# Second cross-attention: smaller packs first, one combined normalisation, row tile 0 projected first, and each quad's queries made inside the loop

## The chip, the cores and the metric

One Trainium2 chip, and of it one core. The time is microseconds (us) of device time of one launch; a lower one is better. Five engines work from queues of their own, each in program order, and meet only at semaphores: PE (TensorE, matmuls), DVE (VectorE), ACT (ScalarE), POOL (GpSimd) and SP (SyncE, which here only issues DMAs and waits).

## What is computed

A perceiver block with x of shape (16, 64, 256) and a context of shape (16, 1601, 256). It has six stages in a row: a top-k cross-attention, a retention stage, a mixture-of-experts feed-forward, a **second cross-attention**, random features, and a tree-routed feed-forward. Only the second cross-attention is touched:

```python
def _L1_xattn_ref(q, k, v, norm_w, norm_b, norm1_w, norm1_b, Wq, bq, Wk, bk, Wv, bv, Wo, bo):
    B, L, D_MODEL, H = (4, 512, 256, 16)
    E = D_MODEL // H
    ...
    qn = layernorm(q, norm_w, norm_b)
    kn = layernorm(k, norm_w, norm_b)
    vn = layernorm(v, norm_w, norm_b)
    Q = (qn @ Wq + bq).reshape(b, l, H, E)
    K = (kn @ Wk + bk).reshape(b, s, H, E)
    V = (vn @ Wv + bv).reshape(b, s, H, E)
    scale = 1.0 / jnp.sqrt(jnp.asarray(E, Q.dtype))
    scores = jnp.einsum('blhe,bshe->bhls', Q, K)
    A = jax.nn.softmax(scale * scores, axis=-1)
    O = jnp.einsum('bhls,bshd->blhd', A, V)
    O = O + Q
    out = jnp.transpose(O, (0, 2, 1, 3)).reshape(b, l, H * E)
    return layernorm(out, norm1_w, norm1_b) @ Wo + bo + out
```

It is called with `_layernorm(x)` as q, so the queries pass two layer norms in a row, and with the context as both k and v.

## The kernel before

**Tiling.** The stage is the function `phase_heads_read`. x lies as 8 row tiles of 128 rows (NT = 8, D = 256, KD = 2 halves of D). There are B = 16 batches of L = 64 query rows each; a batch's context of S = 1601 rows is cut into four quarters (`SPANS`, 512, 384, 384 and 322 columns) and 13 chunks of up to 128 rows. The 16 heads go in two halves m = 0, 1 of 8 heads; one (batch, m) is a **quad**, n = 2b + m, 32 in all. In a quad four groups j of two heads each are worked on.

**What a quad needs.** A matmul of two fp32 factors is made exact enough from a high and a low part. `stage` holds keys as high and low; `load_stack` has SP copy them into `stack` by 12 DMAs, three for each j (high, low, high, 32 partitions each), and copy the queries (high, high, low) from the DRAM tensor `queries` into the tile `queries` by 3 DMAs. Both tiles have two slots, chosen by m. PE then runs 16 `find_top` matmuls (L1485; four spans for each j), DVE reduces each to a maximum (`take_top`, L1733), and the 4 x 128 maxima come back by `shift` (L1492) and `take_shift` (L1748) as four extra rows of the queries; the rows at partitions 96 to 99 of the stack are marks that select them. After that come 13 `score` chunks (L1503), `exp` on ACT (L1637) into `ring`, sums of the ring on POOL (L1389) and DVE (L1762), and `weigh` (L1519).

**Order of the loop.** It is written out by hand, in seven groups g of two chunks. While quad n is scored, PE finds the tops of quad n+1 (`TOP_AT`: in g = 2, 3, 4) and makes keys and values of the next batch (`fill`, L1462 and L1470, spread by `FILL_AT`). `find_top` v = 0 waits for all three queries DMAs; v = 0, 4, 8, 12 wait for the three stack DMAs of their j. SP runs `batch`: `load_stack(b, 1)` (which waits for all scores of the quad before, whose slot it is free to write one quad on), `load_rows(b + 2, 3)`, `load_stack(b + 1, 0)`, the row scales (`load_stds`) and three quarters of rows three batches ahead. SP is in order too: a wait holds back all DMAs behind it.

**Opening.** One DMA brings all parameters (`pd`, 2328 columns). DVE and ACT run the first norm (`d_ln0`), the weights of keys and values are scaled, centred and split, and the second norm (`d_ln1`) runs over the result of the first. PE then transposes all 8 tiles (L164), fills run, and after fill 1 all tiles are projected at once (L216). ACT and DVE build the masked, halved queries of all 16 batches in two pieces (`by_head(ownH)`, L1677, and `by_head(ownL)`, L1812); `ownH` sits in slot 1 of `stack`, `ownL` in `ring`. SP stores both (2 x 2 MB) to DRAM, waits for them, copies the marks and calls `load_stack(0, 0)`. Only then come the 16 first `find_top`s and the loop.

## Time and profile before

| | us |
|---|---|
| median of 3 runs | 1737.65 |
| their lowest and highest | 1735.89, 1746.78 |
| the profiled execution | 1746.88 |
| its span | 1745.0 |
| PE busy in the span | 1479.3 |
| DVE busy | 1032.5 |
| ACT busy | 644.8 |
| POOL busy | 611.9 |

The profile is of one execution, and its span begins with that execution's first work; a time such as 602.97 is us from there. The second cross-attention opens at 517.76 (first DMA), its first exponential starts at 602.97, and the last load of a quad is issued at 1391.13. TensorE's clock has two levels here, 1.2 and 2.4 GHz, shown as a share: 0.50 and 1.00. A row of a timeline gives start, duration, engine, line and operation, how many instructions are merged, and in brackets how long the engine was idle before and what ended that.

### The profile page before, as it was taken

To read this page: it belongs to the slowest core of one execution; us is meant where nothing else is said; L and a number is where in the kernel's file an instruction comes from. 1 tells how busy PE (TensorE), PEld (TensorE's weight loads), DVE (VectorE), ACT (ScalarE), POOL (GpSimd) and SP (SyncE) were. 2 spreads that over 40 slices of the span, in tenths; PEclk is the share of its full clock that TensorE was granted. 3 is DMA by queue.
4 is the path that set the end of the run, shared out by engine and by line. 5 is a ranking of instruction groups with operands and counts; after the bars stand their busy time and mean duration, and the time that the engine had idled before them with its cause. 6 is when DMAs were issued, how large, how long until landed. Compare 5 with 4: busy or idle time off the path is not lost. (4 is left out here: it accounts for less than half of the span.)

```text
span 1745.0 us, 29559 instructions
## 1 busy us (share of the span) xinstructions
PE 1479.3 (85%) x11422; PEld 1150.0 (66%) x11422; DVE 1032.5 (59%) x1937; ACT 644.8 (37%) x1210; POOL 611.9 (35%) x478
## 2 busy tenths in 40 slices
PE   7878767848945799999999999999999983669997
...
GB/s 358 175 260 274 235 1 91 191 1 1 193 40 101 249 140 159 123 148 180 157 143 162 138 143 157 162 132 167 108 151 123 78 47 63 61 109 1 1 0 24
DMA packets 100390, 220.09 MB, mean 126 GB/s; under 512 B 10065, under 2 KB 73889, under 8 KB 98721
## 3 DMA queue, kind: packets, MB, share of 16 engines
...
## 5 line engine op out<-in xcount | busy, mean ns | idle before, releaser
L1637 ACT ACTIVATE d_ring<-psum 128x512 f32<-128x512 f32 (+1 forms) x416 | 229.3, 595 | 301.9 <-PE psum L1503 229.1
L1389 POOL TENSOR_TENSOR d_ring<-d_ring 128x512 f32<-128x512 f32 x224 | 293.2, 1309 | 121.8 <-ACT d_ring L1637 105.5
L1733 DVE TENSOR_REDUCE d_top<-psum 128x1 f32<-128x400 f32 (+2 forms) x512 | 270.1, 569 | 101.4 <-PE psum L1485 96.7
L1503 PEld LDWEIGHTS psum<-d_queries,d_stack 100*128 100x128 f32 (+1 forms) x1664 | 212.0, 196 | 35.3 <-issue 34.5
L1503 PE MATMUL psum<-d_queries,d_stack 100*128 100x128 f32 (+1 forms) x1664 | 233.0, 284 | 1.0 <-DVE d_queries L1748 0.9
L1485 PE MATMUL psum<-d_stack,d_queries 96*128 96x400 f32 (+1 forms) x512 | 185.4, 419 | 40.9 <-DVE d_top L1733 31.9
L1356 POOL TENSOR_TENSOR d_rowsT<-d_raw,d_rowsT 128x1024 fp32r<-128x1024 f32 (+1 forms) x64 | 126.5, 1980 | 199.8 <-ACT d_rowsT L1608 199.8
L1470 PE MATMUL psum<-d_wv,d_rowsT 128*128 128x256 f32 (+1 forms) x1248 | 175.2, 292 | 7.3 <-DVE d_stage L1724 7.3
L1470 PEld LDWEIGHTS psum<-d_wv,d_rowsT 128*128 128x128 f32 (+1 forms) x1248 | 167.3, 194 | 7.9 <-DVE d_stage L1724 7.9
L1724 DVE SCALAR_TENSOR_TENSOR d_stage<-psum,d_bk,d_stage 128x384 fp32r<-128x384 f32 (+2 forms) x128 | 81.0, 633 | 143.0 <-ACT d_stage L1617 143.0
L1462 PE MATMUL psum<-d_rowsT,d_wk 128*128 128x384 f32 (+2 forms) x768 | 160.5, 359 | 3.0 <-POOL d_rowsT L1356 2.5
L1485 PEld LDWEIGHTS psum<-d_stack,d_queries 96*128 96x128 f32 x512 | 92.0, 200 | 92.7 <-DVE d_top L1733 75.7
L1519 PE MATMUL psum<-d_ring,d_val 128*32 128x128 f32 (+1 forms) x3328 | 151.2, 290 | 1.8 <-ACT d_ring L1637 1.8
L1462 PEld LDWEIGHTS psum<-d_rowsT,d_wk 128*128 128x128 f32 x768 | 135.2, 195 | 14.1 <-issue 3.4
L970 POOL TENSOR_TENSOR c_partL<-moe_in,c_partH 128x256 fp32r<-128x256 f32 x8 | 5.5, 738 | 386.7 <-ACT c_partH L1058 386.7
L1762 DVE TENSOR_TENSOR d_ring<-d_ring 128x512 f32<-128x512 f32 (+1 forms) x128 | 122.9, 961 | 13.9 <-ACT d_ring L1637 6.5
L1519 PEld LDWEIGHTS psum<-d_ring,d_val 128*32 128x32 f32 (+1 forms) x3328 | 87.2, 113 | 41.4 <-issue 29.4
L1348 POOL TENSOR_TENSOR d_raw<-d_raw,d_rowstd 128x768 f32<-128x768 f32 (+2 forms) x60 | 106.6, 1788 | 18.0 <-DMA d_raw<-ctxT_dram 18.0
L1617 ACT ACTIVATE d_stage<-psum,d_bk 128x384 fp32r<-128x384 f32 (+2 forms) x128 | 76.1, 595 | 63.6 <-PE psum L1462 63.6
L2012 POOL TENSOR_TENSOR f_wL<-f_raw,f_wH 128x1024 fp32r<-128x1024 f32 x12 | 31.2, 2607 | 188.3 <-ACT f_wH L2138 188.3
L2222 DVE TENSOR_SCALAR f_own<-psum,pf 128x512 f32<-128x512 f32 x48 | 36.1, 751 | 91.0 <-ACT f_ownH L2165 91.0
L1622 ACT ACTIVATE d_val<-psum 128x512 f32<-128x512 f32 x96 | 57.5, 599 | 86.2 <-PE psum L1470 86.1
...
## 6 DMA issues: line engine op xcount, KB each, us to landing
d_stack<-d_stage SPq DMA_DIRECT2D x384, 200.2 KB, 4.2
...
```

The lines of the kernel that those rows point to most:

```text
L1348: eng.tensor_tensor(raw[:, :, s0:s0 + w], raw[:, :, s0:s0 + w], rowstd[:, s0:s0 + w].unsqueeze(1).broadcast_to([P, KD, w]), ALU.mult)\
L1356: eng.tensor_tensor(rowsT[:, 1, :, s0:s0 + w], raw[:, :, s0:s0 + w], rowsT[:, 0, :, s0:s0 + w].bitcast(F32), ALU.subtract).then_inc(sig("d ...
L1389: pool.tensor_tensor(sums[:, 0, m, :], first, ring[:, slot_of(u, m, c), :], ALU.add)\
L1462: last = pe.matmul(ps[:, bank, 0:w], wk[:, a, k, j * P:(j + 1) * P], rowsT[:, c, k, s0:s0 + w], start=((k, a, c) == steps[0]), stop=((k, a ...
L1470: last = pe.matmul(ps[0:w, bank, (c % 2) * D:(c % 2 + 1) * D], rowsT[:, f, k, c * P:c * P + w], wv[:, e, k, :], start=((k, e, f) == steps[ ...
L1485: pe.matmul(ps[:, M_BANK + v % 2, 0:w], queries[0:96, m, j, :], stack[0:96, m, j, s0:s0 + w], start=True, stop=True).then_inc(sig("d_top_p ...
L1503: last = pe.matmul(ps[0:w, S_BANK + (m + c) % 2, j * P:(j + 1) * P], stack[0:STACKED, m, j, c * P:c * P + w], queries[0:STACKED, m, j, :], ...
L1519: last = pe.matmul(ps[32 * g:32 * g + 32, V_BANK + m, 0:P], val[0:w, u, c, f:f + 32], ring[0:w, slot_of(u, m, c), g * P:(g + 1) * P], star ...
L1637: act.activation(ring[0:w, slot_of(u, m, c), :], ps[0:w, S_BANK + (m + c) % 2, :], ACT.Exp)\
L1724: dve.scalar_tensor_tensor(stage[:, m, 1, s0:s0 + w], ps[:, bank, 0:w], bk[:, m:m + 1], stage[:, m, 0, s0:s0 + w].bitcast(F32), ALU.add, A ...
L1733: dve.tensor_reduce(top[:, m, v:v + 1], ps[:, M_BANK + v % 2, 0:min(w, S - s0)], X, ALU.max)\
L1762: dve.tensor_tensor(sums[0:w, 1, m, :], first, ring[0:w, slot_of(u, m, c), :], ALU.add)\
```

## The change

The change touches the second cross-attention alone. What it does:

- The pack `pd` becomes three, loaded apart: `pd0` (keys' and values' weights and biases, 1034 columns), `pd1` (the queries' weights, 514) and `pd2` (what the end needs, 780).
- The two norms become one: from the first norm's variance and reciprocal deviation, three small steps (`spread`), one square root and one reciprocal give a `gain`, and x is normalised once with it, tile 0 first.
- Row tile 0 (batches 0 and 1) is turned and projected alone, ahead of the fills; tiles 4 to 7 and 1 to 3 follow between the fills. The first 16 `find_top`s stand between the last four fills instead of behind them.
- DVE and POOL share the scaling and low parts of the first batch's rows; the copy of the marks moves behind them on POOL.
- The masked queries are made one quad at a time: POOL's `own_queries` (128 x 128 product), ACT's `own_highs` (copy, and the bias on a 128 x 64 piece of QT), POOL's `own_lows`, and SP's `store_own`, a 128 KB DMA to DRAM. For batch b + 1 this happens while batch b is scored (`OWN_AT` = 4, `GATHER_AT` = 6).
- In `load_stack` the 12 stack DMAs are issued first, then a wait for the quad's store, then the 3 queries DMAs.
- DVE's add of chunk 1 moves from g = 1 to g = 0.

The diff, cut to what matters:

```diff
-    "pd": [("n_wcol", 2), ("n_bcol", 2), ("n1_wcol", 2), ("n1_bcol", 2),
-           ("l1_wq", 512), ("l1_wk", 512), ("l1_wv", 512), ("l1_wo", 512), ("l1_bq", 2), ("l1_bk", 2),
-           ("l1_bv", 2), ("l1_bo", 256), ("head_mask", 8), ("parity", 2)],
+    "pd0": [("n_wcol", 2), ("n_bcol", 2), ("parity", 2), ("l1_bk", 2), ("l1_bv", 2), ("l1_wk", 512), ("l1_wv", 512)],
+    "pd1": [("l1_bq", 2), ("l1_wq", 512)],
+    "pd2": [("n1_wcol", 2), ("n1_bcol", 2), ("l1_wo", 512), ("l1_bo", 256), ("head_mask", 8)],
...
+    SHIFT_AT, DEN_AT, HEADS_AT, OWN_AT, GATHER_AT = 5, 0, 1, 4, 6
...
                 n = 2 * b + m
                 wait(sp, "d_lows", 4 * n + 4)
                 wait(sp, "d_s_ps", NC * (n - 1))
-                for part, r in ((0, 0), (0, 32), (1, 64)):
-                    sp.dma_start(queries[r:r + 32, m, :, :].bitcast(F32),
-                                 drams["queries"][part, m, :, bass.ds(b * P, P)].rearrange("(j r) n -> r j n", r=32))\
-                      .then_inc(sig(f"d_queries_in{m}"), 16)
                 for j in range(4):
                     for part, r in ((0, 0), (1, 32), (0, 64)):
                         sp.dma_start(stack[r:r + 32, m, j, :].bitcast(F32),
                                      stage[32 * j:32 * j + 32, m, part, :].bitcast(F32))\
                           .then_inc(sig(f"d_stack_in{m}{j}"), 16)
+                sp.wait_ge(sig(f"d_own_out{m}"), 16 * (b + 1))
+                for part, r in ((0, 0), (0, 32), (1, 64)):
+                    sp.dma_start(queries[r:r + 32, m, :, :].bitcast(F32),
+                                 drams["queries"][n, part].rearrange("(j r) n -> r j n", r=32))\
+                      .then_inc(sig(f"d_queries_in{m}"), 16)
+
+            def store_own(b, m):
+
+                n = 2 * b + m
+                wait(sp, "d_own", n + 1)
+                sp.dma_start(drams["queries"][n].rearrange("c p n -> p c n"), ownHL[:, m, :, :].bitcast(F32))\
+                  .then_inc(sig(f"d_own_out{m}"), 16)
...
                     load_rows(b + 2, 3)
+                if now and after:
+                    store_own(b + 1, 0)
                 if after:
                     load_stack(b + 1, 0)
                 if ahead:
                     load_stds(b + 3)
                     for q in range(3):
                         load_rows(b + 3, q)
-
+                if after:
+                    store_own(b + 1, 1)
+
+            load_params("pd0")
             load_stds(0)
-            for q in range(4):
+            load_rows(0, 0)
+            load_params("pd1")
...
                 load_rows(0, q)
+            load_params("pd2")
+            store_own(0, 0)
             load_stds(1)
...
-            sp.wait_ge(sig("d_own"), 4)
-            for part, src in enumerate((ownH, ownL)):
-                sp.dma_start(drams["queries"][part].rearrange("m p n -> p m n"),
-                             src[:, 0:2 * QW].rearrange("p (m n) -> p m n", m=KD).bitcast(F32))\
-                  .then_inc(sig("d_own_out"), 16)
-            sp.wait_ge(sig("d_own_out"), 32)
...
+            def own_queries(b, m):
+
+                n = 2 * b + m
+                cols = slice(b * L, (b + 1) * L)
+                if n == 0:
+                    for s, v in both(sig, "d_Q0", 1):
+                        pool.wait_ge(s, v)
+                elif n == 4:
+                    for s, v in both(sig, "d_QT"):
+                        pool.wait_ge(s, v)
+                pool.tensor_tensor(own[:, m, :, :], QT[:, m, cols].unsqueeze(1).broadcast_to([P, 2, L]), half[:, :, :],
+                                   ALU.mult).then_inc(sig("d_own_whole"), 1)
+
+            def own_lows(b, m):
+
+                n = 2 * b + m
+                wait(pool, "d_ownH", n + 1)
+                pool.tensor_tensor(ownHL[:, m, 1, :], own[:, m, :, :].rearrange("p h q -> p (h q)"),
+                                   ownHL[:, m, 0, :].bitcast(F32), ALU.subtract).then_inc(sig("d_own"), 1)
...
+            for q in (2, 3):
+                scale_rows(pool, 0, q, f"d_scaled0{q}")
+            own_queries(0, 0)
+            own_lows(0, 0)
+            for q in (2, 3):
+                low_rows(pool, 0, q, f"d_rowlows0{q}")
+            own_queries(0, 1)
+            own_lows(0, 1)
+            pool.wait_ge(sig("d_own"), 2)
             pool.tensor_copy(stack[MARKS, 0, :, :],
...
                             if c in POOL_ADDS:
                                 add(b, u, m, c)
+                        if fills and g == OWN_AT:
+                            own_queries(b + 1, m)
                         if g == GATHER_AT and (m or not first):
                             gather_heads(*before(b, m))
+                        if fills and g == GATHER_AT:
+                            own_lows(b + 1, m)
                         if rows and m == 0:
                             for q in SCALE_AT.get(g, ()):
...
-            turn_tensor(pe, core, "d_natT", nat, 0, [(sig("d_ln1_out"), True)])
...
+            def turn(tiles, first, tag, v):
+
+                pe.wait_ge(sig("d_ln1_out"), tiles[-1] + 1)
+                for k in range(KD):
+                    for i, t in enumerate(tiles):
+                        last = pe.transpose(ps[:, first + k, i * P:(i + 1) * P], nat[:, t, k * P:(k + 1) * P],
+                                            core.p("ident"))
+                    last.then_inc(sig(f"{tag}_ps"), 1)
+
+            def project(tiles, first, src, v, tag):
+
+                for s, n in both(sig, src, v):
+                    pe.wait_ge(s, n)
+                cols = slice(tiles[0] * P, (tiles[-1] + 1) * P)
+                for m in range(KD):
+                    for k in range(KD):
+                        last = pe.matmul(ps[:, first + m, 0:len(tiles) * P], core.w("l1_wq")[:, k, m * P:(m + 1) * P],
+                                         natT[:, k, cols], start=(k == 0), stop=(k == KD - 1))
+                    last.then_inc(sig(f"{tag}_ps"), 1)
...
+            turn(TILES[0], 0, "d_n0", 1)
+            pe.wait_ge(sig("d_pd1_in"), 16)
+            project(TILES[0], 2, "d_n0", 1, "d_Q0")
+            pe.wait_ge(sig("d_weights"), 4)
+            pe.wait_ge(sig("d_shifts"), 1)
+            for n in range(4):
+                fill(0, 0, n)
+            turn(TILES[1], 0, "d_natT", 1)
+            for s, v in both(sig, "d_Q0", 1):
+                pe.wait_ge(s, v)
+            turn(TILES[2], 2, "d_natT", 2)
+            for n in range(4, 6):
+                fill(0, 0, n)
+            project(TILES[1], 0, "d_natT", 1, "d_QT")
+            for n in range(6, 8):
+                fill(0, 0, n)
+            project(TILES[2], 2, "d_natT", 2, "d_QT")
+            for n in range(8, 11):
                 fill(0, 0, n)
             for s, v in both(sig, "d_QT"):
                 pe.wait_ge(s, v)
-            for v in range(TOPS):
-                find_top(0, 0, v)
+            for n in range(11, FILLS):
+                fill(0, 0, n)
+                for v in range(4 * (n - 11), 4 * (n - 11) + 4):
+                    find_top(0, 0, v)
             shift(0, 0)
             pe.wait_ge(sig("d_marks"), 1)
...
+                        if fills and g == OWN_AT:
+                            own_highs(b + 1, m)
+
+            def own_highs(b, m):
+
+                n = 2 * b + m
+                cols = slice(b * L, (b + 1) * L)
+                wait(act, "d_own_whole", n + 1)
+                wait(act, f"d_own_out{m}", 16 * b)
+                act.activation(ownHL[:, m, 0, :], own[:, m, :, :].rearrange("p h q -> p (h q)"), ACT.Copy)\
+                   .then_inc(sig("d_ownH"), 1)
+                act.activation(QT[:, m, cols], QT[:, m, cols], ACT.Identity, bias=bv[:, m:m + 1])\
+                   .then_inc(sig("d_QT_bv"), 1)
...
+            act.wait_ge(sig("d_spread"), 3)
+            act.activation(std2[:, :], spread[:, :], ACT.Sqrt).then_inc(sig("d_std2"), 1)
+            for n, dst in enumerate((wk, wv)):
                 act.wait_ge(sig("d_centred"), n + 1)
...
+            turn(TILES[0], 0, "d_n0", 1)
             act.wait_ge(sig("d_pad"), 1)
...
+            project(TILES[0], 2, "d_Q0", 1)
+            rows_of(0, 1)
+            own_highs(0, 0)
+            act.wait_ge(sig("d_shifts"), 1)
+            take_fill(0, 0, 0)
...
+            dve.tensor_tensor(spread[:, :], moments[:, :, 1], rstd[:, :], ALU.mult).then_inc(sig("d_spread"), 1)
+            dve.wait_ge(sig("d_spread"), 1)
+            dve.tensor_tensor(spread[:, :], spread[:, :], rstd[:, :], ALU.mult).then_inc(sig("d_spread"), 1)
+            dve.wait_ge(sig("d_spread"), 2)
+            dve.tensor_scalar(spread[:, :], spread[:, :], EPS, None, ALU.add).then_inc(sig("d_spread"), 1)
+            for n in range(2):
...
+                dve.scalar_tensor_tensor(scaled[:, n, :, :], ps[:, V_BANK + 1 + n, 0:D].unsqueeze(1).broadcast_to([P, KD, D]),
+                                         -1.0 / D, scaled[:, n, :, :], ALU.mult, ALU.add).then_inc(sig("d_centred"), 1)
+                if n == 0:
+                    dve.wait_ge(sig("d_std2"), 1)
+                    dve.reciprocal(std2[:, :], std2[:, :]).then_inc(sig("d_rstd2"), 1)
+                    dve.wait_ge(sig("d_rstd2"), 1)
+                    dve.tensor_tensor(gain[:, :], std2[:, :], rstd[:, :], ALU.mult).then_inc(sig("d_gain"), 1)
+                    dve.wait_ge(sig("d_gain"), 1)
+                    dve.tensor_scalar(nat[:, 0, :], x[:, 0, :], moments[:, 0, 0:1], gain[:, 0:1],
+                                      ALU.subtract, ALU.mult).then_inc(sig("d_ln1_out"), 1)
...
+            low_rows(dve, 0, 0, "d_rowlows00")
+            project(TILES[0], 2, "d_Q0", 1)
+            low_rows(dve, 0, 1, "d_rowlows01")
+            for t in range(1, NT):
+                dve.tensor_scalar(nat[:, t, :], x[:, t, :], moments[:, t, 0:1], gain[:, t:t + 1],
+                                  ALU.subtract, ALU.mult).then_inc(sig("d_ln1_out"), 1)
...
-                        for c in GROUPS[g - 1] if g else ():
-                            if c in VECTOR_ADDS:
+                        for c in (1,) if g == 0 else GROUPS[g - 1]:
+                            if c in VECTOR_ADDS and (g == 0 or c > 1):
                                 add(b, u, m, c)
```

SP's order in the middle of the loop (`d_stack` and `d_queries` are the two loads of a quad, `d_raw` and `d_rowstd` a later batch's rows and scales), before:

```order
L1280 DMA d_raw<-ctxT_dram 128x2x321
L1290 DMA d_queries<-queries_dram 32x4x128 x3
L1295 DMA d_stack<-d_stage 32x1602 x12
L1272 DMA d_rowstd<-row_stds_dram 128x1602
L1280 DMA d_raw<-ctxT_dram 128x2x512
L1280 DMA d_raw<-ctxT_dram 128x2x384 x2
L1290 DMA d_queries<-queries_dram 32x4x128 x3
```

and now:

```order
L1283 DMA d_raw<-ctxT_dram 128x2x321
L1307 DMA queries_dram<-d_ownHL 128x2x128
L1294 DMA d_stack<-d_stage 32x1602 x12
L1299 DMA d_queries<-queries_dram 32x4x128 x3
L1273 DMA d_rowstd<-row_stds_dram 128x1602
L1283 DMA d_raw<-ctxT_dram 128x2x512
L1283 DMA d_raw<-ctxT_dram 128x2x384 x2
L1307 DMA queries_dram<-d_ownHL 128x2x128
L1294 DMA d_stack<-d_stage 32x1602 x12
L1299 DMA d_queries<-queries_dram 32x4x128 x3
```

The three queries DMAs went from ahead of the twelve stack DMAs to behind them, and one store stands ahead of each load.

DVE's order around the first tops of a quad (L1762, now L1924, is the add into the ring's sums; L1724, now L1886, the low part of a key fill; TENSOR_REDUCE the tops), before:

```order
L1762 TENSOR_TENSOR d_ring<-d_ring 65x512
L1724 SCALAR_TENSOR_TENSOR d_stage<-psum,d_bk,d_stage 128x512
L1724 SCALAR_TENSOR_TENSOR d_stage<-psum,d_bk,d_stage 128x384 x2
L1770 RECIPROCAL pd<-psum 128x128
L1773 TENSOR_TENSOR pd<-psum,pd 128x128
L1724 SCALAR_TENSOR_TENSOR d_stage<-psum,d_bk,d_stage 128x322
L1762 TENSOR_TENSOR d_ring<-d_ring 128x512
L1733 TENSOR_REDUCE d_top<-psum 128x1 x16
```

and now:

```order
L1924 TENSOR_TENSOR d_ring<-d_ring 65x512
L1886 SCALAR_TENSOR_TENSOR d_stage<-psum,d_bk,d_stage 128x512
L1886 SCALAR_TENSOR_TENSOR d_stage<-psum,d_bk,d_stage 128x384
L1924 TENSOR_TENSOR d_ring<-d_ring 128x512
L1886 SCALAR_TENSOR_TENSOR d_stage<-psum,d_bk,d_stage 128x384
L1932 RECIPROCAL pd<-psum 128x128
L1935 TENSOR_TENSOR pd<-psum,pd 128x128
L1886 SCALAR_TENSOR_TENSOR d_stage<-psum,d_bk,d_stage 128x322
L1895 TENSOR_REDUCE d_top<-psum 128x1 x16
```

The one full-width add moved from right ahead of the tops to between the key fills.

PE's order in the opening, from the column sums (256 wide) to the first tops, before:

```order
L1443 MATMUL psum<-pd,d_ones 128x256 x4
L164 MATMUL psum<-pk,d_ring 128x128 x16
L1462 MATMUL psum<-d_rowsT,d_wk 128x512 x6
L1462 MATMUL psum<-d_rowsT,d_wk 128x384 x6
L216 MATMUL psum<-d_val,pd 128x512 x8
L1462 MATMUL psum<-d_rowsT,d_wk 128x384 x6
L1462 MATMUL psum<-d_rowsT,d_wk 128x322 x6
L1470 MATMUL psum<-d_wv,d_rowsT 128x256 x48
```

and now (L1628 turns, L1639 projects, L1516 and L1524 fill):

```order
L1497 MATMUL psum<-pd 128x1 x8
L1628 MATMUL psum<-pk,d_ring 128x128 x2
L1639 MATMUL psum<-d_val,pd 128x128 x4
L1516 MATMUL psum<-d_rowsT,d_wk 128x512 x6
L1516 MATMUL psum<-d_rowsT,d_wk 128x384 x12
L1516 MATMUL psum<-d_rowsT,d_wk 128x322 x6
L1628 MATMUL psum<-pk,d_ring 128x128 x14
L1524 MATMUL psum<-d_wv,d_rowsT 128x256 x24
L1639 MATMUL psum<-d_val,pd 128x512 x4
L1524 MATMUL psum<-d_wv,d_rowsT 128x256 x24
L1639 MATMUL psum<-d_val,pd 128x384 x4
```

Two transposes and four narrow projections stand ahead of the first fill in place of sixteen transposes, and the rest of both went behind the first four fills.

## Rows read from the trace of the kernel before

**Rows 1.** Who waited for whom, stretch 660 to 1400 us (total, times, longest).

```profile
ACT d_ring L1637 <- DVE d_ring L1762: 66.4, 28, 2.5
PEld psum L1485 <- DVE d_top L1733: 65.8, 151, 1.8
...
PE psum L1485 <- DMA d_stack<-d_stage: 1.7, 1, 1.7
```

**Rows 2.** Timeline of SP's queue in the loop: start, us, what was issued.

```profile
627.25 1.27 SPq L1290 DMA_DIRECT2D d_queries<-queries_dram  x3
...
989.51 1.26 SPq L1290 DMA_DIRECT2D d_queries<-queries_dram  x3
990.81 10.57 SPq L1295 DMA_DIRECT2D d_stack<-d_stage  x12
...
1015.33 1.29 SPq L1290 DMA_DIRECT2D d_queries<-queries_dram  x3
...
1040.74 1.27 SPq L1290 DMA_DIRECT2D d_queries<-queries_dram  x3
...
1068.99 1.28 SPq L1290 DMA_DIRECT2D d_queries<-queries_dram  x3
...
1391.13 1.27 SPq L1290 DMA_DIRECT2D d_queries<-queries_dram  x3
```

**Rows 3.** Lines L1295 and L1290, whole run: issue in ns, landing in us.

```profile
L1295 SPq DMA_DIRECT2D d_stack<-d_stage x384: 507/950/1746, 583.2 to 1402.2; - x192
...
DMA to landing us min/median/max: 2.7/4.2/8.0
...
DMA to landing us min/median/max: 1.9/2.0/7.4
```

**Rows 4.** Timeline of all engines around the first tops of two quads.

```profile
998.82 0.58 PE L1485 MATMUL psum<-d_stack,d_queries 96*128 96x402 f32 x2
...
999.40 2.49 DVE L1762 TENSOR_TENSOR d_ring<-d_ring 128x512 f32<-128x512 f32 x1
...
1002.43 0.93 PE L1485 MATMUL psum<-d_stack,d_queries 96*128 96x400 f32 x2 [1.61 <-DVE d_top L1733]
...
1014.70 0.46 POOL L1398 TENSOR_TENSOR pd<-pd,d_mask 128x128 f32<-128x128 f32 x1
...
1015.24 1.62 POOL L1402 TENSOR_TENSOR d_QT<-d_QT,pd 128x64 f32<-128x64 f32 x2
...
1024.65 0.58 PE L1485 MATMUL psum<-d_stack,d_queries 96*128 96x402 f32 x2
```

**Rows 5.** Busy time by stretch: PE, PEld, DVE, ACT, POOL, granted clock, DMA share, GB/s.

```profile
569.00:573.00 4.00, 4.00 (x25) 4.00 (x24) 0.00 (x0) 1.19 (x2) 0.00 (x0) 0.64 1.01 418
...
1064.80:1068.00 3.20, 3.20 (x28) 2.64 (x27) 0.55 (x1) 1.57 (x3) 2.23 (x4) 0.50 0.31 108
```

**Rows 6.** Timeline of the opening, PE, SP, POOL and ACT.

```profile
539.60 3.68 PE L164 MATMUL psum<-pk,d_ring 128*128 128x128 f32 x16 [7.50 <-DVE d_ring L138]
545.79 4.82 PE L1462 MATMUL psum<-d_rowsT,d_wk 128*128 128x512 f32 x12 [2.51 <-POOL d_rowsT L1356]
550.40 7.51 PE L216 MATMUL psum<-d_val,pd 128*128 128x512 f32 x16
...
566.98 8.11 PE L1470 MATMUL psum<-d_wv,d_rowsT 128*128 128x256 f32 x48 [7.13 <-DVE d_stage L1724]
...
588.17 0.60 PE L1485 MATMUL psum<-d_stack,d_queries 96*128 96x402 f32 x2 [3.67 <-DMA d_stack<-d_stage]
...
566.42 0.37 SPq L1319 DMA_DIRECT2D queries_dram<-d_stack  x1
...
583.19 10.61 SPq L1295 DMA_DIRECT2D d_stack<-d_stage  x12
...
523.15 5.52 POOL L1366 CAST d_stack<-pk 4x6408 fp32r<-4x6408 f32 x1
...
602.97 0.60 ACT L1637 ACTIVATE d_ring<-psum 128x512 f32<-128x512 f32 x1 [14.04 <-PE psum L1503]
```

209 lines of the change are left out of this document (116 added, 93 removed).

## The prediction

> **What bounds the kernel now.** I read, in this order, the waits of the loop, SP's queue, the landing times of its two loads, and the engines around the first tops of a quad. In the stretch from 660 to 1400 us PE hardly waits for anything but the maxima: weight loads of the tops wait 65.8 us for DVE, and a stack DMA was late once, 1.7 us [rows 1]. The loop is bound by PE, and its loads arrive in time. How much in time is the question here. SP issues three queries DMAs, then twelve stack DMAs, as soon as the scores of the quad before are done; call that moment the boundary [rows 2]. From the boundary at 989.51 the first top starts at 998.82, from that at 1015.33 it starts at 1024.65 [rows 2, 4]: 9.3 us each. The three queries DMAs are issued in 1.26 us and land 2.0 us after issue; the twelve stack DMAs are issued in 10.57 us and each lands 4.2 us after issue [rows 2, 3]. So today the queries are there 3 us after the boundary, the stack of j = 0 after 1.3 + 2.6 + 4.2 = 8.1 us at most (three of twelve issues are 2.6), 1.2 us ahead of its use. The mean quad is (1391.13 - 627.25) / 29 = 26.34 us; single ones are 1040.74 - 1015.33 = 25.4 (scores of m = 0), 1015.33 - 989.51 = 25.8 (m = 1) and, with TensorE at 0.50 in its last part, 1068.99 - 1040.74 = 28.25 [rows 2, 5].
>
> **The change, part by part.**
>
> *Queries behind the stack, in each quad.* `find_top` v = 0 needs all three queries DMAs. They now start behind the twelve others: 10.57 us after the boundary, their last issue starts 0.86 later (two thirds of 1.26), and it lands 2.0 us after that at best: 13.4. The 2.0 was measured on a queue that was empty. Behind the stack's packets it will be more; if it is as long as the stack's own 4.2, the queries are there at 15.6. I take 14.5, nearer the busy queue, and keep 13.4 and 15.6 for the range. PE stands in its queue at the first top 9.3 us after the boundary, so it waits 5.2 us (4.1 to 6.3), and behind it wait the fills, weighs and scores of the rest of the quad, hence exp, hence the next boundary, from which the next load starts. The delay doesn't run out: each quad pays it anew. The Trainium skill's DMA page (DMA: Bandwidth & Descriptors, Queues, rings and completion order) says that each DMA engine consumes descriptors in ring order, which speaks against putting small urgent transfers behind large ones. By that rule alone the landing would be near 4.2 and the wait 6.3; by the queries' own row it would be 4.1. No row of the kernel before shows the two loads in this order.
>
> *What PE gets back.* In the m = 1 quad PE waits 1.61 us at the third top, because DVE's add of chunk 1 (2.49 us from 999.40) ran just ahead of the reductions [rows 4]. That add moves to g = 0, and during the new wait DVE is done with all else, so I subtract 1.8 in the m = 1 quad (1.61 and the short waits beside it) and 0.25 in the m = 0 quad. ACT's waits for the same add (66.4 us, 28 times [rows 1]) go as well, but PE's scores didn't stand behind them, so they give nothing more.
>
> *The clock.* After PE's idle 7.13 us it worked at half clock from 566.98; the stretch 569 to 573 is granted 0.64, thus 2.9 us at 0.50, in all 4.9 us of work at half speed, a loss of 2.4 [rows 5, 6]. The 28.25 us quad lost 2.45 against the 25.8 one. A wait of 5 us in each quad will bring the 0.50 back each time; I charge 2.2 a quad, and nothing at the lower end. The mean quad holds 26.34 - 25.6 = 0.74 of such loss already. The Trainium skill (TensorE: Matmul & The Clock Gate, HAM oscillation) describes this: waits for DMA in each round of a loop let the clock fall each time. The rows agree for one gap; without the clock the sum below would be 68 us smaller.
>
> *Queries made in the loop.* POOL gets two 128 x 128 products a quad, 0.46 us each by its product of that size, ACT two short copies, SP one 128 KB store [rows 4]. POOL is 35% busy over the span and its adds run ahead of exp's need, so the products lie beside PE's work: 0. If POOL had no slack they would cost 0.92 x 31 = 29 us. One wait is new: SP issues `store_own(b + 1, 1)` ahead of `load_stack(b + 1, 1)`, and it needs `own_lows` behind `gather_heads` on POOL. In the quad before 1015.33 that gather ran from 1014.70 and its last product ended at 1016.86 [rows 4], so the store could wait until about 2 us past the boundary, with the whole load behind it. Since PE's wait comes earlier in that quad and lets POOL catch up, I charge 0.5 in every second quad, between 0 and 3.
>
> *The sum for the loop.* An m = 1 quad had 16.5 us from first top to boundary, an m = 0 quad 16.1. Now a pair takes (14.5 + 16.5 - 1.8) + (14.5 + 0.5 + 16.1 - 0.25) + 2 x 2.2 = 64.45 in place of 2 x 26.34 = 52.68: 11.8 more. 31 quads look for the tops of a next one, 15.5 pairs: **+182 us**.
>
> *The opening.* Off the path ahead of the first fill go the wait for the second norm (7.50), 14 of 16 transposes (3.2 of 3.68) and the wait for POOL's low rows (2.51); four narrow projections come in (4 of 128 columns for 8 of 512, 0.9 of 7.51): 12.3 earlier [rows 6]. Behind the first fill PE's 7.13 (DVE's low parts stood behind the masked queries of all batches) and 3.67 (queries stored, read back, then the stack) go, 3.2 of transposes come in, and four fills slip between the tops, worth up to 4. That is 24. SP's own path gives the same: first fill near 533.5, four key fills and their lows some 10 us, the marks' copy on POOL (5.52) now behind the low rows, then 10.61 of stack and 3 of queries: about 563, when PE gets to its first top. I take 25 us earlier for the first exponential (578 for 602.97), between 15 and 32. Smaller packs lie in this; pd0 is waited for a little less, and pd2 is there long before its use.
>
> *Together:* 182 - 25 = +157. On the profiled execution's 1746.88 that is 1904. That execution lies 9.2 above the median of 1737.65, so I put it at **1895 us**.
>
> **Rivals.**
> - *The stack's issue is quick enough (other side, faster).* The shortest stack issue took 0.507 us [rows 3]. If all twelve did, the queries would be there at 6.1 + 0.9 + 2.0 = 9.0, below the 9.3 at which PE comes. That is where it decides: a mean issue below 0.53 us. Then nothing is lost, the moved add gives 1.8 + 0.25 a pair, 32 us, and the time is 1738 - 25 - 32 = 1681. Against it: the median issue is 0.95.
> - *PE catches up.* The wait is there, but most is made good because DVE, ACT and POOL stand ready: say 3 us a quad remain, clock and all, 93 - 25 = +68, 1806. For it: PE waits 65.8 us for DVE in 28 quads, 2.3 a quad. Against it: that is all there is to gain.
> - *The load itself starts late.* `store_own` holds the load 2 to 3 us past the boundary in each m = 0 quad, the queries land at 15.6, and the clock stays low longer: 18 us a pair, 280 - 20 = +260, 1998.
> - *The change does nothing to the time.* The 25 us and the loop's loss would have to cancel at 0.8 us a quad; no row points there.
>
> **How the numbers follow.** My forecast, each quad waiting 4 to 6.3 us with the clock falling in most: 0.72, giving 1820 to 1985. PE catches up (1700 to 1820): 0.12. Late load (over 1985): 0.10. Quick issue (faster): 0.05. Cancelling: 0.01. The lower end of the forecast is a wait of 4.1, no clock loss and an opening that gives 30 (1738 + 98 - 30 = 1806, rounded up since all three at once is unlikely); the range of 1815 to 1990 leaves out two in ten. About 1% is what a measurement of this kernel can tell from no change. Faster by more: 0.05; within: 0.02; slower: 0.93.
>
> **What would show it.** In the profile of the changed kernel: PE's first top of a quad waits for `d_queries`, 4 to 6 us, some 31 times, 150 us in all; boundaries 32 us apart; granted clock in the loop well under 0.95; the first exponential near 578. Wrong would be: first tops that come 9.3 us after the boundary as before (then the quick issue is right), the waits there but quads under 29 us (PE catches up), or stack DMAs that start more than 1 us after the last score (late load). An exponential later than 588 would put the opening's term wrong.

## The result, and the profile after

The changed kernel takes 1911.37 us (median of 4 runs, 1900.3 to 1918.3) beside 1742.22 for the kernel before in the same session: a ratio of 1.095, with a 95% interval of 1.085 to 1.105. It is slower by 169 us; forecast were 157.

The waits of PE first. In [rows 1] they were waits for DVE; in the loop of after a new one leads them (columns: engine, line and what it waited for: us in total, times, longest; stretch from 640 to 1590 us):

```profile
PEld psum L1539 <- DMA d_queries<-queries_dram: 160.2, 29, 9.8
PE psum L1539 <- DMA d_queries<-queries_dram: 156.1, 29, 9.7
```

L1539 is the matmul of `find_top`. The same wait over the whole execution, from the view of the queries' DMA (three a quad, 96 in all), with the time from issue to landing:

```profile
L1299 SPq DMA_DIRECT2D d_queries<-queries_dram x96: 431/956/1020, 568.0 to 1562.1; - x96
...
  PEld psum L1539: 170.0, 31
...
DMA to landing us min/median/max: 1.9/2.6/3.5
```

170.0 us in 31 waits are 5.5 us for each quad that has a next one; the longest, 9.8, is the one in the quad before the last. One such quad, first SP's queue, which answers to [rows 2]:

```profile
1064.46 0.38 SPq L1307 DMA_DIRECT2D queries_dram<-d_ownHL  x1
1066.42 10.57 SPq L1294 DMA_DIRECT2D d_stack<-d_stage  x12
1077.04 2.47 SPq L1299 DMA_DIRECT2D d_queries<-queries_dram  x3
1079.55 0.43 SPq L1273 DMA_DIRECT2D d_rowstd<-row_stds_dram  x1
1080.02 12.93 SPq L1283 DMA_DIRECT2D d_raw<-ctxT_dram  x3
1096.76 0.37 SPq L1307 DMA_DIRECT2D queries_dram<-d_ownHL  x1
1097.22 3.70 SPq L1294 DMA_DIRECT2D d_stack<-d_stage  x5
```

The queries go out 10.6 us after the boundary, and the next boundary is 1097.22 - 1066.42 = 30.8 us later, where [rows 2] have 25.4 and 25.8. On PE, beside [rows 4]:

```profile
1074.79 1.11 PE L1557 MATMUL psum<-d_queries,d_stack 100*128 100x128 f32 x8
1081.09 1.03 PE L1539 MATMUL psum<-d_stack,d_queries 96*128 96x402 f32 x2 [5.19 <-DMA d_queries<-queries_dram]
1081.92 2.76 PE L1524 MATMUL psum<-d_wv,d_rowsT 128*128 128x256 f32 x12
1084.48 0.65 PE L1539 MATMUL psum<-d_stack,d_queries 96*128 96x400 f32 x2
```

PE is idle for 5.19 us. The first top comes 14.67 us after the boundary instead of 9.3. The 12 matmuls of a fill behind it take 2.76 us, where a quad of e8 (below) has 1.58 for them at full speed. The windows (columns: stretch, its length, busy time and instructions of PE, PEld, DVE, ACT, POOL, then granted clock, share of DMA, GB/s) show why, and the last of them what it makes of the loop:

```profile
1078.00:1080.00 2.00, 0.00 (x0) 0.00 (x0) 0.00 (x0) 0.00 (x0) 2.00 (x3) 0.50 0.80 184
1082.00:1084.00 2.00, 2.00 (x11) 2.00 (x10) 0.88 (x2) 0.00 (x0) 1.71 (x2) 0.50 0.95 314
1084.00:1086.00 2.00, 2.00 (x23) 1.36 (x21) 1.01 (x2) 0.60 (x1) 0.00 (x0) 0.81 0.93 350
1086.00:1088.00 2.00, 2.00 (x16) 1.91 (x15) 1.44 (x4) 1.02 (x2) 0.35 (x1) 1.00 0.03 12
640.00:1340.00 700.00, 578.54 (x5525) 484.95 (x5526) 353.39 (x611) 291.71 (x536) 398.13 (x351) 0.88 0.52 128
```

The same stretch of the kernel before, where the clock is 0.96 and PE is busy for 92 us more:

```profile
640.00:1340.00 700.00, 670.41 (x6725) 556.63 (x6726) 444.26 (x749) 343.02 (x599) 475.87 (x377) 0.96 0.60 147
```

**Where the time went.** I split both profiled executions (1745.0 and 1916.5 of span) at the last score of a quad, the 66-row chunk that ends each quad.

| part | before | after | difference |
|---|---|---|---|
| start of the stage | 517.76 | 522.01 | +4.3 |
| to the last score of the first quad | 109.4 | 94.2 | -15.2 |
| 30 quads from there | 789.8 (26.33 each) | 967.3 (32.24 each) | +177.5 |
| the last quad | 11.7 | 19.6 | +7.9 |
| the rest | 316.4 | 313.4 | -2.9 |

This *mean quad*, over the same 30 quads, is the measure used below. It comes from one profiled execution of each version, and that one isn't always the median one: it lies 6.9 us above its median in after, 2.4 above in e12, 3.2 below in e8 and 8.6 below in e6. Spread over 30 quads, this makes a difference of two mean quads uncertain by up to 0.5.

The last quad is a case of its own. In the profiled executions of after, e1, e9, e10, e11 and e12 it takes 19.5 to 19.6 us, in the other eight 11.3 to 11.7. So 8 us of a difference between two versions can lie there and not in the loop.

### The profile page after: what moved, and what is told of

Same layout as the page of the kernel before. It is cut to its first block and busy times, and to the rows that moved or that the text cites. A ratio compares the mean times of both kernels' runs of the same rounds, so it can differ in the third digit from the quotient of the medians.

```text
span 1916.5 us, 29745 instructions
## 1 busy us (share of the span) xinstructions
PE 1538.0 (80%) x11430; PEld 1205.8 (63%) x11430; DVE 1006.6 (53%) x1914; ACT 654.8 (34%) x1272; POOL 625.1 (33%) x542
## 3 DMA queue, kind: packets, MB, share of 16 engines
q8 instruction: 87, 1.43, 0.3%
## 5 line engine op out<-in xcount | busy, mean ns | idle before, releaser
L1439 POOL TENSOR_TENSOR d_ring<-d_ring 128x512 f32<-128x512 f32 x224 | 286.7, 1280 | 282.3 <-ACT d_ring L1725 268.4
L1539 PE MATMUL psum<-d_stack,d_queries 96*128 96x400 f32 (+1 forms) x512 | 195.6, 450 | 176.4 <-DMA d_queries<-queries_dram 160.1
L1539 PEld LDWEIGHTS psum<-d_stack,d_queries 96*128 96x128 f32 x512 | 100.2, 227 | 223.2 <-DMA d_queries<-queries_dram 170.0
L1524 PE MATMUL psum<-d_wv,d_rowsT 128*128 128x256 f32 (+1 forms) x1248 | 206.8, 326 | 0.0
L1524 PEld LDWEIGHTS psum<-d_wv,d_rowsT 128*128 128x128 f32 (+1 forms) x1248 | 200.5, 230 | 0.8 <-issue 0.5
L1370 POOL TENSOR_TENSOR d_rowsT<-d_raw,d_rowsT 128x768 fp32r<-128x768 f32 (+2 forms) x62 | 117.3, 1893 | 199.9 <-ACT d_rowsT L1696 199.7
L1516 PE MATMUL psum<-d_rowsT,d_wk 128*128 128x384 f32 (+2 forms) x768 | 160.6, 359 | 4.4 <-DVE d_rowsT L1370 2.2
L1573 PE MATMUL psum<-d_ring,d_val 128*32 128x128 f32 (+1 forms) x3328 | 159.2, 303 | 0.0
L1516 PEld LDWEIGHTS psum<-d_rowsT,d_wk 128*128 128x128 f32 x768 | 135.5, 195 | 15.2 <-DVE d_stage L1886 3.0
L1886 DVE SCALAR_TENSOR_TENSOR d_stage<-psum,d_bk,d_stage 128x384 fp32r<-128x384 f32 (+2 forms) x128 | 81.1, 633 | 106.0 <-ACT d_stage L1705 105.9
L1573 PEld LDWEIGHTS psum<-d_ring,d_val 128*32 128x32 f32 (+1 forms) x3328 | 91.6, 118 | 45.6 <-issue 40.6
L1362 POOL TENSOR_TENSOR d_raw<-d_raw,d_rowstd 128x768 f32<-128x768 f32 (+2 forms) x62 | 116.8, 1895 | 5.4 <-DMA d_raw<-ctxT_dram 5.3
L1924 DVE TENSOR_TENSOR d_ring<-d_ring 128x512 f32<-128x512 f32 (+1 forms) x128 | 104.1, 814 | 23.0 <-ACT d_ring L1725 15.5
## 6 DMA issues: line engine op xcount, KB each, us to landing
moe_w<-moe_w_dram SPq DMA_DIRECT2D x16, 1024.0 KB, 10.6
```

The source lines that it names most:

```text
L1362: eng.tensor_tensor(raw[:, :, s0:s0 + w], raw[:, :, s0:s0 + w], rowstd[:, s0:s0 + w].unsqueeze(1).broadcast_to([P, KD, w]), ALU.mult)\
L1370: eng.tensor_tensor(rowsT[:, 1, :, s0:s0 + w], raw[:, :, s0:s0 + w], rowsT[:, 0, :, s0:s0 + w].bitcast(F32), ALU.subtract).then_inc(sig(do ...
L1439: pool.tensor_tensor(sums[:, 0, m, :], first, ring[:, slot_of(u, m, c), :], ALU.add)\
L1516: last = pe.matmul(ps[:, bank, 0:w], wk[:, a, k, j * P:(j + 1) * P], rowsT[:, c, k, s0:s0 + w], start=((k, a, c) == steps[0]), stop=((k, a ...
L1524: last = pe.matmul(ps[0:w, bank, (c % 2) * D:(c % 2 + 1) * D], rowsT[:, f, k, c * P:c * P + w], wv[:, e, k, :], start=((k, e, f) == steps[ ...
L1539: pe.matmul(ps[:, M_BANK + v % 2, 0:w], queries[0:96, m, j, :], stack[0:96, m, j, s0:s0 + w], start=True, stop=True).then_inc(sig("d_top_p ...
```

## The experiments

All ran in four groups, each beside the kernel before, which had medians of 1739.02 (e1 to e4), 1745.46 (e5 to e8), 1740.33 (e9, e10) and 1742.48 (e11, e12). None leaves out any work of the kernel. What they gave together:

| version | median us | ratio to before, 95% | mean quad |
|---|---|---|---|
| before | 1742 | 1 | 26.33 |
| after | 1911.4 | 1.085 to 1.105 | 32.24 |
| e3, before, queries behind the stack | 1939.7 | 1.108 to 1.123 | 32.29 |
| e10, after, add of chunk 1 at g = 1 | 1917.6 | 1.101 to 1.105 | 32.29 |
| e8, after, PE kept busy in the wait | 1864.8 | 1.066 to 1.076 | 30.50 |
| e1, after, queries ahead of the stack | 1742.1 | 0.996 to 1.003 | 26.91 |
| e2, after, queries behind j = 0 | 1709.3 | 0.977 to 0.987 | 25.81 |
| e4, e2, add of chunk 1 at g = 1 | 1734.0 | 0.994 to 1.000 | 26.48 |
| e5, queries behind j = 0 and 1 | 1762.1 | 1.008 to 1.017 | 27.25 |
| e9, before, add of chunk 1 at g = 0 | 1709.8 | 0.978 to 0.986 | 24.90 |
| e6, e2 and an early store | 1688.5 | 0.966 to 0.975 | 24.87 |
| e7, e1 and an early store | 1689.7 | 0.967 to 0.976 | 25.11 |
| e11, e5 and an early store | 1698.2 | 0.971 to 0.983 | 25.30 |
| e12, behind j = 0 to 2, early store | 1810.5 | 1.030 to 1.048 | 29.17 |

**Is it the place of the queries in the queue?** e3 puts that one part of the change into the kernel before; e1 and e2 take it out of the kernel after.

e3, in `load_stack` of the kernel before:

```diff
-                for part, r in ((0, 0), (0, 32), (1, 64)):
-                    sp.dma_start(queries[r:r + 32, m, :, :].bitcast(F32), ...
                 for j in range(4):
                     for part, r in ((0, 0), (1, 32), (0, 64)):
                         sp.dma_start(stack[r:r + 32, m, j, :].bitcast(F32), ...
+                for part, r in ((0, 0), (0, 32), (1, 64)):
+                    sp.dma_start(queries[r:r + 32, m, :, :].bitcast(F32), ...
```

> The kernel before with one move alone: the three queries DMAs behind the twelve stack DMAs. If this order alone makes the loss, the loop grows as in the changed kernel (170 us, and 13 in the last two quads), the opening loses about 3 and nothing waits for a store (8 less): 1742 + 178 = 1920, between 1890 and 1940. Rival: it takes the new layout, the store or the in-loop queries as well: under 1850.

It takes 1939.65 us, and its PE waits in the loop as that of after does (640 to 1340 us):

```profile
PE psum L1485 <- DMA d_queries<-queries_dram: 116.9, 22, 6.2
```

After has 115.3, 22 and 5.9 there, and the mean quads are 32.29 and 32.24. So the order of 15 DMAs alone makes the whole loss of the loop, with no new work anywhere. e3 is even slower than after, since it has not the shorter opening: its first quad ends 24.3 us later.

e2, in the kernel after (the wait for the store moves along):

```diff
                 for j in range(4):
                     for part, r in ((0, 0), (1, 32), (0, 64)):
                         sp.dma_start(stack[...
+                    if j == 0:
+                        sp.wait_ge(sig(f"d_own_out{m}"), 16 * (b + 1))
+                        for part, r in ((0, 0), (0, 32), (1, 64)):
+                            sp.dma_start(queries[...
-                sp.wait_ge(sig(f"d_own_out{m}"), 16 * (b + 1))
-                for part, r in ((0, 0), (0, 32), (1, 64)):
-                    sp.dma_start(queries[...
```

> The changed kernel with one move: the wait and the three queries DMAs stand behind the three stack DMAs of j = 0 instead of behind all twelve. If the late queries are what the change costs, PE's 330 us of waits for d_queries go to under 20, the first top of a quad is again about 9.3 us after the boundary, the granted clock of the loop returns to 0.95 or more, and the time is 1742 - 16 (opening, as the changed kernel shows it) - 6 (the queries wait inside the opening) - 30 (the moved add) = 1690, between 1675 and 1710. Rival: the queries made in the loop (POOL, ACT, store) cost something themselves: then 1705 to 1740. Rival: the loop is slow for another reason than the queries' place: over 1800.

e1, the same lines ahead of all twelve:

> The changed kernel with the wait for the store and the queries DMAs ahead of all twelve stack DMAs. In every second quad the store is issued at the boundary itself and must have landed (about 2 us) before the load begins. If that wait stands on the path, stack j = 0 lands about 10.5 us after the boundary where PE comes at 9.3: 1 to 1.5 us in 15 quads, so 15 to 25 us above the variant with the queries behind j = 0: about 1710. If it has slack, both are equal within 5 us.

e2 takes 1709.34 us: all of the loss gone, and faster than before, but 19 above the 1690 that I expected. e1 takes 1742.11, some 30 more than expected, and 8 of them can be its last quad. Most of its quads alternate between 23.8 and about 30.8 us, and PE waits for the stack (13 times, 36.6 us). In its SP queue a load goes out 1.89 us behind a store:

```profile
955.67 0.37 SPq L1307 DMA_DIRECT2D queries_dram<-d_ownHL  x1
957.56 1.88 SPq L1294 DMA_DIRECT2D d_queries<-queries_dram  x3
959.48 10.61 SPq L1299 DMA_DIRECT2D d_stack<-d_stage  x12
```

The last score before it had ended at 951.52. So the load was 6.0 us late: 4.2 by which the store itself was late, and 1.9 for its landing, which the queries' load waits for. That is the "late load" rival, and e2 has it in a smaller form.

**The store that holds the load.** In e2 the last score of a quad ended at 938.06. POOL's queue around it, then SP's:

```profile
921.73 2.40 POOL L1371 TENSOR_TENSOR d_rowsT<-d_raw,d_rowsT 128x1024 fp32r<-128x1024 f32 x1 [10.03 <-ACT d_rowsT L1697]
...
927.11 5.55 POOL L1440 TENSOR_TENSOR d_ring<-d_ring 128x512 f32<-128x512 f32 x4
932.62 0.46 POOL L1402 TENSOR_TENSOR d_own<-d_QT,d_half 128x128 f32<-128x128 f32 x1
...
938.39 1.42 POOL L1454 TENSOR_TENSOR d_QT<-d_QT,pd 128x64 f32<-128x64 f32 x2
939.77 0.45 POOL L1409 TENSOR_TENSOR d_ownHL<-d_own,d_ownHL 128x128 fp32r<-128x128 f32 x1
```

```profile
940.25 0.37 SPq L1308 DMA_DIRECT2D queries_dram<-d_ownHL  x1
940.71 1.78 SPq L1294 DMA_DIRECT2D d_stack<-d_stage  x3
942.54 2.27 SPq L1300 DMA_DIRECT2D d_queries<-queries_dram  x3
```

POOL first waits 10.03 us for ACT's high part of the rows, then works without a gap, and `own_lows` comes last: at 940.22, 2.2 us past the last score. The load goes out behind the store, 2.65 us after the last score; in the next such quad it is 4.6 (last score 989.29, load 993.92). I call this delay the hold. It is there in 14 of the 15 loads behind an m = 1 quad, with 1.6 to 4.6 us, and it is the longer the shorter that quad was: 4.6 behind quads of 23.8 us, 3.2 behind 25.3, 1.6 behind 26.7. e6 makes the own queries two groups earlier:

```diff
-    SHIFT_AT, DEN_AT, HEADS_AT, OWN_AT, GATHER_AT = 5, 0, 1, 4, 6
+    SHIFT_AT, DEN_AT, HEADS_AT, OWN_AT, LOWS_AT, GATHER_AT = 5, 0, 1, 2, 4, 6
...
-                        if fills and g == GATHER_AT:
+                        if fills and g == LOWS_AT:
                             own_lows(b + 1, m)
```

> The version with the queries behind j = 0, with POOL's and ACT's part of the queries made two groups earlier (g = 2 for the product and the high part, g = 4 for the low part, instead of 4 and 6). In that version every second load goes out 2.7 to 4.6 us after the last score, 0.46 us behind its store, whose low part POOL makes only then. Theory (that hold is what makes the quads of m = 0 last 27.5 to 28.6 us after one of 23.8): the load goes out within 0.1 us, pairs of 51.6 us become about 50.3, 1709 - 20 = 1690 us (1680 to 1700). Rival (the first top has no wait there, so the hold costs nothing and the long quads are DVE's): 1709.

e7 is e1 with the same edit:

> The version with the wait for the store and the queries ahead of all 12 stack DMAs, with the store's work made two groups earlier as in e6. There the load goes out 6 us after the last score in every second quad, and the quad after it lasts 30.8 us. Theory (the held load costs them all): these quads go to 25.8 or less, 1742 - 15 x 4 = 1680 us, between 1670 and 1700, as e6. Rival (the first three stack DMAs behind the queries come too late whatever the store does): 1742, with waits of PE for the stack left.

e6 takes 1688.54 us and e7 1689.71. In e6 the last score of a quad ends at 1227.13 and the load starts at 1227.46, 0.33 later. POOL's, PE's and SP's rows:

```profile
1224.20 0.45 POOL L1409 TENSOR_TENSOR d_ownHL<-d_own,d_ownHL 128x128 fp32r<-128x128 f32 x1
```

```profile
1226.67 0.46 PE L1558 MATMUL psum<-d_queries,d_stack 100*66 100x128 f32 x4
```

```profile
1226.89 0.47 SPq L1308 DMA_DIRECT2D queries_dram<-d_ownHL  x1
1227.46 1.78 SPq L1294 DMA_DIRECT2D d_stack<-d_stage  x3
```

The store here waited for SP's row loads, no longer for POOL. In e7 the hold is shorter, not gone: in nine of its 15 loads behind an m = 1 quad it is 3.2 to 3.4 us, since there the whole load waits for the store to land. One whose last score ended at 629.66:

```profile
629.42 0.47 SPq L1307 DMA_DIRECT2D queries_dram<-d_ownHL  x1
632.86 1.28 SPq L1294 DMA_DIRECT2D d_queries<-queries_dram  x3
```

In these nine the first top comes 9.7 to 10.6 us after the last score, against 10.4 to 13.6 in e1 with its holds of 3.8 to 6.6. By the medians the early store brings e2 20.8 us and e1 52.4, 8 of the latter in the last quad. With it, it matters little whether the queries stand first or behind j = 0.

**How late may they be?** e5 and e11 put the queries behind six stack DMAs, e12 behind nine; the edit is that of e2 with `j == 1` or `j == 2`.

> The changed kernel, with the wait for the store and the three queries DMAs behind the six stack DMAs of j = 0 and 1. Six stack DMAs take 4.7 us to issue, the queries 2.5 and their landing 2.6, so they are there 9.8 to 10.4 us after the last score of the quad before, and PE asks for them after 9.3. Theory (PE pays for how late the queries are, and no more): waits of 0.5 to 1.1 us, up to 3 where the store holds the load back, about 2 us a quad with the clock, 1709 + 62 = 1770 us (1735 to 1810). Rival (the loss is not graded: any wait costs the clock its whole fall): 1840 or more. Rival (what costs is the queue's state and not the lateness): 1709, as with the queries behind j = 0.

> Queries behind the stack DMAs of j = 0 and 1, with the early store of e6. With the late store of e5 the loads that go out on time have their queries there 9.1 us after the last score, and PE comes to them at 9.4 without a wait, while the loads held for 4.6 us make PE wait 4.0. Theory (only the sum of place in the queue and hold counts): no waits are left, 1689 us, as e6, up to 1705. Rival (six DMAs ahead cost by themselves): nearer 1750.

> Queries behind the nine stack DMAs of j = 0 to 2, with the early store. Nine issues take 7.5 us, the last queries DMA starts 1.7 later and lands after 2.7: 11.9 us after the last score, so PE waits 2.5 us in each quad. Theory A (a wait costs its length and no clock at this size): 1689 + 31 x 2.5 = 1767 us. Theory B (it costs its length and as much clock as the waits of 5.2 us, 1.75 a quad): 1689 + 31 x 4.25 = 1821 us. Rival (DVE and ACT make the wait good): under 1740.

e5 took 1762.11 us, and one trace shows both cases. Last scores ended at 1284.04 and 1315.44; SP's rows, then PE's first tops:

```profile
1288.66 4.81 SPq L1294 DMA_DIRECT2D d_stack<-d_stage  x6
1293.52 2.55 SPq L1300 DMA_DIRECT2D d_queries<-queries_dram  x3
...
1315.52 4.65 SPq L1294 DMA_DIRECT2D d_stack<-d_stage  x6
1320.21 2.58 SPq L1300 DMA_DIRECT2D d_queries<-queries_dram  x3
```

```profile
1297.58 1.04 PE L1540 MATMUL psum<-d_stack,d_queries 96*128 96x402 f32 x2 [3.98 <-DMA d_queries<-queries_dram]
...
1324.84 0.58 PE L1540 MATMUL psum<-d_stack,d_queries 96*128 96x402 f32 x2
```

The load held for 4.6 us makes PE wait 3.98, and its quad takes 31.4; the load on time has its top 9.4 us after the last score with no wait. e11 removes the hold and comes to 1698.15, with waits of 6.2 us in all from 640 to 1340. That is 10 above e6, of which 8 can be the last quad; the mean quad is 0.4 longer. Six DMAs are where the slack ends. e12 comes to 1810.53 (1798.1 to 1825.0): PE waits 88.4 us for the queries in 31 quads, 2.85 each. The mean quad is 29.17 - 24.87 = 4.30 above that of e6, so 1.45 come on top of the wait; by the medians it is some 3.9, and 1.1 on top. With the last quad's 8 us taken off, 1810 becomes 1803: nearer to theory B (1821) than to theory A (1767).

**What the clock adds.** e8 keeps PE busy in the wait of after:

```diff
                 if v == 0:
+                    wait(pe, "d_shift", n)
+                    wait(pe, "d_top", TOPS * n - 1)
+                    for _ in range(22):
+                        pe.matmul(ps[:, M_BANK, 0:P], ones[:, :], ones[:, :], start=True, stop=True)
                     wait(pe, f"d_queries_in{m}", 48 * (b + 1))
```

> The changed kernel, and ahead of the wait for the queries 22 matmuls of ones (128 x 128) into a bank that is free, so that PE is busy through most of its 5.2 us of waiting; the data of the kernel and the wait are the same. Theory (2.2 us of each quad's loss is the clock that falls behind the wait): the clock stays at 1.00 behind it, 31 x 2.2 = 68 less, about 1843 us (1825 to 1865). Rival (the clock falls for another reason, or its fall is covered by waits for DVE): 1911. If the 22 matmuls outlast the wait, they cost their own time.

It takes 1864.80 us, 47 less than after (42 by the two ratios), though it does more work and starts its tops no earlier. One quad, and the loop's window:

```profile
1081.18 5.13 PE L1537 MATMUL psum<-d_ones 128*128 128x128 f32 x44
1086.49 0.64 PE L1543 MATMUL psum<-d_stack,d_queries 96*128 96x402 f32 x2 [0.19 <-DMA d_queries<-queries_dram]
1086.97 1.58 PE L1524 MATMUL psum<-d_wv,d_rowsT 128*128 128x256 f32 x12
```

```profile
640.00:1340.00 700.00, 685.35 (x6859) 587.80 (x6858) 375.28 (x650) 308.60 (x566) 422.37 (x372) 0.98 0.55 133
```

The last score had ended at 1071.78, so the first top is at +14.7 us as in after, but the fill behind it takes 1.58 us instead of 2.76, and the loop's clock is 0.98 instead of 0.88. The mean quad falls from 32.24 to 30.50: by the two profiles the clock costs 1.74 us a quad. But these lie 57 us apart where the medians lie 47 and the ratios give 42; with the excess taken off the loop the price is 1.2 to 1.4. All these are less than the 2.2 that I expected. Another 8 us of the gain are the last quad's, 11.4 us in e8 and 19.6 in after. The remaining 30.50 - 24.87 = 5.63 is about the time for which PE's program stands still for its own work: 5.13 of ones and some 0.5 of waiting.

**The moved add.** e4 is e2 with DVE's add of chunk 1 back at g = 1, e9 the kernel before with the add at g = 0, e10 the kernel after with it at g = 1. The edit in all three is this one or its reverse:

```diff
-                        for c in GROUPS[g - 1] if g else ():
-                            if c in VECTOR_ADDS:
+                        for c in (1,) if g == 0 else GROUPS[g - 1]:
+                            if c in VECTOR_ADDS and (g == 0 or c > 1):
```

> As the variant with the queries behind j = 0, and DVE's add of chunk 1 back at g = 1. My sum gave the moved add 1.8 + 0.25 us a pair of quads, 32 us in all: then this is 1722 against 1690. Rival: PE's 1.6 us wait at the third top has another cause or is made up for later: both within 8 us.

> The kernel before, with DVE's add of chunk 1 moved from g = 1 to g = 0 and nothing else. Theory of the prediction (PE's wait of 1.61 us at the third top of each m = 1 quad and 0.25 in the others goes): 32 less; by the two versions that differ in this add alone (1734.0 and 1709.3) 25 less. So 1739 - 25 = 1714 us, between 1700 and 1725. Rival (it was worth 25 only where the loads were held back by the store): about 1739.

> The changed kernel, with DVE's add of chunk 1 back at g = 1. Theory (PE's 5.2 us of waiting gives DVE the time for the add, so that the move is worth nothing as long as the queries are late): 1911 us, within 10. Rival (the move is worth its 25 to 32 us here too): 1936 to 1943.

e9 takes 1709.76 us, 30.6 less than the kernel before, by this move alone; most of its m = 1 quads last 23.8 us, where before had 25.8. Its loop gains more than that (1.43 us a quad by the two profiles), and 8 us are lost again in the last quad. e4 takes 1734.00, 24.7 more than e2.

In e4 the hold answers to the quad's length too. Its queries are made late in the loop as in e2 and PE has no long wait, and yet most loads are on time: the hold is 3.2 us behind the three m = 1 quads that took 25.8 us, 0.5 behind the three of 27.2, and 0.1 behind those of 28.4 and more. With e2's holds this makes one series: POOL is ready some 28 us after the quad's start, and a shorter quad waits for it. The moved add shortens the quad to 23.8, so it brings out the hold: its worth is 24.7 us with the hold in the way (e2 against e4), and 30.6 without (e9). e10 takes 1917.64, and its mean quad (32.29) is that of after (32.24): where PE stands still for 5 us, DVE has the time for the add wherever it is put. By the ratios e10 isn't told apart from after. PE's waits for DVE at the tops (640 to 1340 us) say the same: 28.9 us in before, 5.3 in after, 4.9 in e10.

## Why the prediction was right, point by point

Forecast were 1895 us in 1815 to 1990; measured are 1911.4. The likeliest case held. The two profiled executions lie 171.5 us apart, 14.5 more than the forecast 157: the stage starts 4.3 later, the opening gives 9.8 less, the last quad takes 7.9 more, and the loop (-4.5) and the rest (-2.9) take less. Of its steps:

- **What bounds the loop** and **queries behind the stack**: the first top was forecast 14.5 us after the boundary, it came at 14.67; a wait of 5.2 was forecast, 5.19 is that of the quad shown, 5.5 the mean. Its parts were mixed differently: the issue of the three queries DMAs took 2.47 us and not 1.26, and the landing 2.6. That is 0.6 above the 2.0 of [rows 3] and far from the stack's 4.1. The other reading, a landing as long as the stack's, would have given a wait of 6.3; the longest from 640 to 1340 us is 6.0. The prediction took that reading from the Trainium skill (DMA: Bandwidth & Descriptors, Queues, rings and completion order), which says that each DMA engine takes its descriptors in ring order; that section says nothing of how long the landing is, and the trace, which has each DMA's issue and landing alone, doesn't show that order.
- **It doesn't run out**: 31 waits, and the boundaries 32.24 us apart where 64.45 / 2 = 32.2 were forecast. The loop's +182 was +177.5 in 30 quads, and 5.9 a quad as forecast.
- **The clock**: forecast 2.2 a quad, measured 1.2 to 1.75 (e8 against after). In the quad shown PE works at 0.50 from 1081.09 to about 1084.8 (0.81 is the mean of 1084 to 1086), 3.7 us; with PE busy through the wait, the loop's clock is 0.98. The Trainium skill (TensorE: Matmul & The Clock Gate, HAM oscillation) describes a loop whose waits for DMA let the clock fall in each round, so that the work behind starts slow; the trace of after agrees with it, with 0.50 behind the wait and 0.88 over the loop.
- **What PE gets back**: the value was near, the reason was wrong. I credited 1.8 + 0.25 a pair to the moved add. In after it is worth nothing (e10); the standstill itself gives DVE its time. Outside of it the move is worth 30.6 us (e9), near the 32 of the rival "quick issue". That the terms add up so well is in part luck. Forecast were 24.6 for a quad without the wait, 5.2 of wait, 2.2 of clock and 0.25 for late loads, 32.2 in all; measured are 24.87 (e6), 5.5, at most 1.74 and nothing, 32.1 in all. Two terms were too small and two too large.
- **Queries made in the loop at no cost**: true for after, where the load was on time (last score 1097.14, load 1097.22), since with PE's wait its m = 1 quads last over 30 us and POOL catches up. Where the m = 1 quads last less than about 28 us, it was wrong: in e2, where many last 23.8, the same work held nearly each second load by 1.6 to 4.6 us and cost 21 us (e2 against e6). The step that failed there is "POOL is 35% busy and has slack"; it has slack on average, but none in the second half of an m = 1 quad, behind its 10.03 us of waiting for ACT. Placed two groups earlier it costs nothing that shows: e6's mean quad is 24.87, and e9's, which makes no queries in its loop, 24.90.
- **The opening**: forecast -25, and the first exponential at 578; it came at 590.78, past the 588 that I had set as the bound. From the stage's start to it there were 68.8 us instead of 85.2, thus -16.4. The step that failed is that I let the queries of the first quad arrive by the time PE was there. They stand behind the twelve stack DMAs here too:

```profile
572.05 0.64 PE L1539 MATMUL psum<-d_stack,d_queries 96*128 96x402 f32 x2 [4.02 <-DMA d_queries<-queries_dram]
```

  With them behind j = 0, e2 has its first exponential at 581.11, 60.4 us after its stage's start at 520.69: -24.8, as forecast. So my term was the size of the opening without its first wait, and 8.4 us of the gain were lost to it: 4.0 are the wait, and 3.8 are what the work from the first top to the first score takes longer. It runs at 0.50 from 575 to 590 in after, and at 1.00 in e2 up to 578:

```profile
575.00:590.00 15.00, 12.24 (x43) 9.07 (x42) 7.20 (x14) 4.22 (x6) 5.58 (x4) 0.50 0.69 191
```

- **The end of the loop** was not in the sum: the quad that makes no more fills reaches its first top early and waits longest, and the last quad ran at half clock.

```profile
1564.30 1.04 PE L1539 MATMUL psum<-d_stack,d_queries 96*128 96x402 f32 x2 [9.69 <-DMA d_queries<-queries_dram]
```

  And the windows from there on, with the clock at 0.50:

```profile
1564.00:1600.00 36.00, 34.61 (x257) 26.45 (x257) 13.33 (x24) 10.15 (x17) 13.88 (x14) 0.50 0.00 1
```

  The last quad took 19.6 us instead of 11.7. In before the clock comes back inside it:

```profile
1420.94:1428.00 7.06, 7.06 (x113) 5.75 (x112) 0.96 (x3) 4.62 (x9) 5.64 (x5) 1.00 0.01 3
```

  I can't put the difference down to the wait: e9 and e11 had 19.5 there without such a wait, and e3 had 11.5 with a quad of 34 us ahead. What decides which of the two it is stays open, and with one trace of each version it isn't known whether it belongs to the version or to the execution.
- **The range**: its lower end, 1738 + 98 - 30, can't be worked out again from its terms. A wait of 4.1 with the clock's loss of before kept gives 95; with that loss gone as well it is 72, and the end 1780. The result doesn't hang on it.

Of the rivals, "quick issue" fell (a stack issue took 10.57 as before), "PE catches up" fell, and "late load" was absent from after but real in e2, e1 and e5, which have the late store and the moved add, and in three loads of e4.

**A faster version.** The change holds two gains and one large loss. Keeping the opening (some 25 us) and the moved add (25 to 31 by the medians) and putting the queries behind j = 0 with the store two groups earlier gives 1688.5 us, 3% below the kernel before.
